# Layer-norm moments of the first stage moved in part from VectorE to GpSimd, with its weight preparation and row stores reordered

## What is computed

```python
h = maximum(_layernorm(x), 0)              # (x - m) / sqrt(v + 1e-5)
Wh = h @ W;  e = leaky_relu(Wh @ a[:128] + (Wh @ a[128:]).T, 0.2)
att = softmax(where(adj > 0, e, -9e15), axis=1)
x = x + gru(att @ Wh, h)                   # gates from w_ih, w_hh, b_ih, b_hh
h = maximum(_layernorm(x), 0)
x = x + adj @ (h @ W1.T + b1)              # adj is 8192 x 8192, zeros and ones
```

## Time and profile before

| | |
|---|---|
| median of 3 runs | 1555.94 us (1554.92 to 1555.95) |
| the profiled execution's own time | 1554.47 us |
| its span | 1552.9 us |
| busy: TensorE | 1485.6 us (96%) |
| busy: VectorE | 1386.0 us (89%) |
| busy: ScalarE | 1369.6 us (88%) |
| busy: GpSimd | 136.2 us (9%) |
| mean DMA rate | 324 GB/s |

### The profile page before, as it was taken

How to read it: one execution, slowest core, us unless ns; L and a number is a source line. 1 busy time by engine, 2 the same in 40 slices (tenths; PEclk the granted TensorE clock), 3 DMA queues, 4 the chain that set the end, 5 groups by cost and what they waited for, 6 DMA issues and landing times.

```text
span 1552.9 us, 35381 instructions
## 1 busy us (share of the span) xinstructions
PE 1485.6 (96%) x13262; PEld 1304.4 (84%) x13262; DVE 1386.0 (89%) x2256; ACT 1369.6 (88%) x1972; POOL 136.2 (9%) x98
## 2 busy tenths in 40 slices
PE   5477999999999999999999999999999999999998
PEld 5356888888888888888888888888888888888887
DVE  8997999999999999999999999997579877766684
ACT  5779999999999999999999999996185998777785
POOL 5000011001100010001000100010000000000000
PEclk9778999999999999999999999999999999999999
DMA  8858999999999999999999999996386999888860
GB/s 314 298 204 332 365 350 360 352 366 353 355 357 370 352 349 353 374 351 357 359 365 345 362 362 355 349 360 265 122 354 238 408 361 352 308 304 310 321 228 16
DMA packets 96380, 502.93 MB, mean 324 GB/s; under 512 B 9599, under 2 KB 38985, under 8 KB 75337
## 3 DMA queue, kind: packets, MB, share of 16 engines
q1 hardware_dynamic: 78328, 444.54, 76.1%
q10 hardware_dynamic: 18000, 57.74, 9.8%
HBM read 418.32 MB, written 83.92 MB: 323 GB/s over the span
## 4 chain that ended last, share of the span: by engine, by line
PE 92%; DVE 5%; ACT 1%; issue 1%; DMA 0%; POOL 0%; DVEq 0%; ACTq 0%
PE ACC L1014 57%; PE ACC L1104 29%; PE GP L1040 2%; PE GP L1043 2%; PE GQ L1061 1%; ACT M L506 1%; DVE M L659 1%; DVE JK L642 1%; DVE TB L733 1%; DVE AE L728 1%; DVE JK L728 1%; PE TG L1027 0%; PE TG L1050 0%; DVE JK L646 0%; DVE M L751 0%
## 5 line engine op out<-in xcount | busy, mean ns | idle before, releaser
L1014 PE MATMUL ACC<-TB,M 128*128 128x258 f16 x8192 | 927.2, 275 | 41.8 <-DVE M L751 30.7
L1014 PEld LDWEIGHTS ACC<-TB,M 128*128 128x128 fp8e4 x8192 | 804.5, 98 | 150.7 <-issue 43.2
L506 ACT ACTIVATE M<-SB,dsteep 128x256 fp8e4<-128x256 f32 x1273 | 526.2, 538 | 0.0
L516 ACT ACTIVATE JK<-X 128x3328 uint8<-128x3328 uint32 x124 | 373.2, 3010 | 0.0
L692 DVE TENSOR_SCALAR Y<-X 128x4096 fp8e4<-128x4096 f32 x128 | 291.9, 2280 | 5.9 <-DMA X<-in_adjb_dram 5.5
L605 ACT ACTIVATE TB<-TB 128x8192 uint8<-128x8192 fp8e4 x32 | 225.0, 7030 | 76.5 <-DVE TB L890 71.7
L1104 PE MATMUL ACC<-WG,X 128*128 128x256 f16 x2048 | 225.5, 273 | 0.0
L1104 PE MATMUL ACC<-WG,TB 128*128 128x256 f16 x2048 | 225.4, 273 | 0.0
L1104 PEld LDWEIGHTS ACC<-WG,X 128*128 128x128 fp8e4 x2048 | 200.4, 98 | 23.2
L1104 PEld LDWEIGHTS ACC<-WG,TB 128*128 128x128 fp8e4 x2048 | 200.4, 98 | 23.1
L743 DVE TENSOR_SCALAR M<-SB,nd 128x256 fp8e4<-128x256 f32 x775 | 213.7, 345 | 0.0
(11 more groups left out here) (145 smaller groups left out, 786.9 us busy)
## 6 DMA issues: line engine op xcount, KB each, us to landing
X<-in_adjb_dram SPq DMA_DIRECT2D x128, 2048.0 KB, 9.8
mask_bytes<-Y SPq DMA_DIRECT2D x128, 512.0 KB, 5.1
M<-in_adjb_dram ACTq DMA_DIRECT2D x24, 1920.0 KB, 9.8
X<-mask_bytes SPq DMA_DIRECT2D x16, 2048.0 KB, 9.5
TB<-mask_bytes SPq DMA_DIRECT2D x16, 2048.0 KB, 9.1
M<-in_adjb_dram ACTq DMA_DIRECT2D x4, 2048.0 KB, 11.9
M<-in_xb_dram SPq DMA_DIRECT2D x8, 512.0 KB, 8.3
h_rows<-M SPq DMA_DIRECT2D x8, 512.0 KB, 3.9
```

The costliest lines, as they stand in the source:

```text
L506: ins = nc.scalar.activation(rows(mask1(c), jj), SB[u][:, :], ACT.Sigmoid, scale=STEEP, bias=dsteep[:, j:j + 1], saturate=False)
L516: nc.scalar.activation(junk[:, 0:SEEN], X[c % 2][:, 0:SEEN].bitcast(u32), ACT.Sign, accum_out=nz[:, bass.ds(k, 1), at:at + 1].rearrange("p ...
L1014: ins = nc.tensor.matmul(A[t][m][:, 0:2 * TW], rows((mask1, mask2)[m](c), jj)[:, t * P:(t + 1) * P], TB[:, c * JC + jj, m, 0:2 * TW], star ...
```

## The change

In the first stage:

1. VectorE aggregates only groups 0 and 1. Groups 2 to 7 get `bn_stats` alone, and GpSimd combines the halves for two groups at a time (`pair_moments`): mean = half the sum of the two means; variance + epsilon = the sum of the two parts over 128, plus epsilon, plus the square of (even mean - mean); then the power on 16 columns.
2. `bn_stats` of groups 2 and 3 runs behind `normalised(0)`, of 4 and 5 behind `normalised(1)`, of 6 and 7 behind `normalised(3)`. The copy into wext stands behind groups 2 and 3.
3. GpSimd prepares the gate weights only when VectorE has normalised all groups (`p_hd` at 16).
4. SP stores the rows of groups 0, 1 and 2 behind columns 9, 11 and 13, those of groups 3 to 7 behind column 15 and ahead of the second adjacency block. The first adjacency block stays behind column 7.
5. The factor TSCALE enters the exponentials as log(TSCALE) in their offset; VectorE's two multiplications of the tables go.
6. Semaphore `d_hh` is shared with the new GpSimd steps (18 increments), so line 770 waits for 18 more; the judging wait of line 941 drops from 3 to 1.

```diff
@@ sync
                 for k in range(16):
                     sp.wait_ge(p_ht, k + 1)
                     sp.dma_start(ht_d[:, k * 512:(k + 1) * 512], hTq[k % 4]).then_inc(p_htout[k % 4], 16)
-                    if k % 2:
-                        q = k // 2
+                    if k == 7:
+                        sp.dma_start(X[0][:, :], adjb[0, :, :]).then_inc(c_in[0], 16)
+                    for q in range(*((k - 9) // 2, (k - 7) // 2) if 9 <= k < 15 and k % 2 else (3, 8 if k == 15 else 3)):
                         sp.dma_start(h_d[:, q * 8:(q + 1) * 8, :], H[:, q * 8:(q + 1) * 8, :]).then_inc(p_hout, 16)
-                    if k in (7, 15):
-                        b = k // 15
-                        sp.dma_start(X[b][:, :], adjb[b, :, :]).then_inc(c_in[b], 16)
+                    if k == 15:
+                        sp.dma_start(X[1][:, :], adjb[1, :, :]).then_inc(c_in[1], 16)
@@ gpsimd
-                for q in range(4):
+                def pair_moments(p):
+                    at = slice(p * 16, p * 16 + 16)
+                    mean_e, part_e, mean_o, part_o = [stx[:, at, i:i + 1].rearrange("p t k -> p (t k)") for i in (1, 2, 4, 5)]
+                    mean = mvx[:, at, 0:1].rearrange("p t k -> p (t k)")
+                    pool.wait_ge(p_st, 2 * p + 2)
+                    nc.gpsimd.tensor_tensor(px[0], mean_e, mean_o, ALU.add).then_inc(p_ag, 1)
+                    nc.gpsimd.tensor_tensor(px[1], part_e, part_o, ALU.add).then_inc(p_ag, 1)
+                    pool.wait_ge(p_ag, p * 6 - 5)
+                    nc.gpsimd.tensor_scalar(mean, px[0], 0.5, None, ALU.mult).then_inc(p_ag, 1)
+                    pool.wait_ge(p_ag, p * 6 - 4)
+                    nc.gpsimd.tensor_scalar(px[1], px[1], 1.0 / F, EPS, ALU.mult, ALU.add).then_inc(p_ag, 1)
+                    pool.wait_ge(p_ag, p * 6 - 3)
+                    nc.gpsimd.tensor_tensor(px[0], mean_e, mean, ALU.subtract).then_inc(p_ag, 1)
+                    pool.wait_ge(p_ag, p * 6 - 1)
+                    nc.gpsimd.tensor_tensor(px[0], px[0], px[0], ALU.mult).then_inc(p_ag, 1)
+                    pool.wait_ge(p_ag, p * 6)
+                    nc.gpsimd.tensor_tensor(sdx[:, at], px[1], px[0], ALU.add).then_inc(p_sd, 1)
+                    pool.wait_ge(p_sd, p + 2)
+                    nc.gpsimd.tensor_tensor(rsx[:, at], sdx[:, at], half[:, 0:1].to_broadcast([P, 16]), ALU.pow).then_inc(
+                        p_rs, 2)
+
+                for q in range(2):
                     deviation(q)
+                pair_moments(1)
                 pool.wait_ge(p_wa, 1)
...
-                for q in range(4, 8):
-                    deviation(q)
+                for p in range(2, 4):
+                    pair_moments(p)
+                pool.wait_ge(p_hd, 16)
                 pool.wait_ge(wt_in, 64)
@@ vector
                 stats(0)
+                stats(1)
                 for q in range(8):
-                    if q < 7:
-                        stats(q + 1)
                     normalised(q)
+                    if q in (0, 1, 3):
+                        for ahead in range(q + q % 2 + 2, q + q % 2 + 4):
+                            halves_stats(ahead)
                     if q == 0:
                         dve.wait_ge(p_wa, 1)
                         nc.vector.tensor_copy(wext[:, 0:2], GP[:, 0:2]).then_inc(p_ab, 1)
@@
-                nc.vector.tensor_scalar(kt[:, 0:1], kt[:, 2:3], -1.0, None, ALU.mult)
-                nc.vector.tensor_scalar(kt[:, 1:2], kt[:, 2:3], -SLOPE, None, ALU.mult).then_inc(p_k, 1)
+                nc.vector.tensor_scalar(kt[:, 0:1], kt[:, 2:3], -1.0, math.log(TSCALE), ALU.mult, ALU.add)
+                nc.vector.tensor_scalar(kt[:, 1:2], kt[:, 2:3], -SLOPE, math.log(TSCALE), ALU.mult, ALU.add).then_inc(p_k, 1)
@@ table_product
                     if i == 0:
-                        for n, table in enumerate((bt, dt_)):
-                            dve.wait_ge(p_exp, n + 1)
-                            nc.vector.tensor_scalar(table, table, TSCALE, None, ALU.mult).then_inc(t_sc, 1)
                         dve.wait_ge(p_one, 2)
                         for b in range(2):
                             dve.wait_ge(p_htout[b], 64)
-                        dve.wait_ge(t_sc, 2)
+                    if i < 2:
+                        dve.wait_ge(p_exp, i + 1)
```

More of the change, by code:

```diff
@@ L1 @@
 from contextlib import ExitStack
+import math
 import concourse.bass as bass
@@ L151, in binary_adjacency @@
         nmx = JK[:, 670:670 + NT]
+        px = [JK[:, 740 + 20 * i:740 + 20 * i + 16] for i in range(2)]
         BG = X1[0].bitcast(bf16)
@@ L206, in binary_adjacency @@
         d_hh, d_hl = sem("d_hh"), sem("d_hl")
+        p_ag = d_hh
         g_sum = p_wa
@@ L638, in _, with halves_stats @@
             def _(dve):
-                def stats(q):
+                def halves_stats(q):
                     dve.wait_ge(p_x[q], 16)
@@ L643, in stats @@
                     ins.then_inc(p_st, 1)
+                def stats(q):
+                    halves_stats(q)
                     dve.wait_ge(p_st, q + 1)
@@ L769, in gate_step @@
                     if halving:
-                        dve.wait_ge(d_hh, qh + 1)
+                        dve.wait_ge(d_hh, 18 + qh + 1)
                         nc.vector.tensor_tensor(HH[:, 1, :], HT[u], HH[:, 0, :], ALU.subtract).then_inc(d_hl, 1)
@@ L940, in judge @@
                 def judge():
-                    dve.wait_ge(k_w, 3)
+                    dve.wait_ge(k_w, 1)
                     nc.vector.tensor_reduce(bad[:, 3:4], GP[:, 0:1], AX.X, ALU.max).then_inc(k_v, 1)
```

## The result

The changed kernel took 1557.97 us in the median of 12 runs (1555.21 to 1560.35), the one before 1556.05 in 12 runs (1554.80 to 1558.05). The ratio is 1.0016, 95% interval [1.0008, 1.0023]: slower by 1.9 us between the medians, 2.5 by the ratio, and so within the 0.2% that the prediction called no change. The profiled execution after is the longest of the twelve, 1560.35 us with a span of 1558.8.

The account below looks back on a forecast made before the run. An entry of some 126 us paced by VectorE, ScalarE and stores, then a TensorE-bound body. Compute side -0.9 us, but late row stores gate the masks: sum +1.4 on 1555.94, forecast 1557.4; 8-in-10 range 1554.7 to 1560.3.

Parts of the forecast that it names:

- The last row store so lands at 47.7 + 5.1 = 52.8: Entry: four row stores moved behind the first adjacency load add 5.1 us at 411 GB/s to the last landing.
- The first masks start at 52.85: everything behind it moves with them: Line 506: masks wait for the last row store, start 1.4 to 1.5 us later than 51.39, and delay everything behind.
- The load: First adjacency load: issued at 28.8, landing at 37.5 as before, with column 12 waiting behind it until 38.25.
- It will run 3.1 us later: Copy at line 672, behind two more groups of statistics: 14.8 instead of 11.64; columns and features start 3.1 us late.
- The pair: GpSimd's moments for two groups: seven small operations at 0.45 us and a power of 1.9, 5.0 us in all.
- the port rule: VectorE and GpSimd share a port: each small operation could wait one multiplication more, 1.9 us a pair, 6.9 in all.
- Saved there: 2.5 us: VectorE's last normalised group: moving the gate weights' preparation away cuts its multiplications from 4.08 to 1.6 us.
- 0.4 is left of the 8: VectorE ends about 8 us sooner, but column 12's wait leaves only 0.4 us of that at the columns' end.
- Dropping the scaling: Table scaling behind the columns: two instructions, 0.49 us, come off the path to the first masks.
- 1 (stores in time): Last row store lands 1.5 us or more sooner, compute side rules: -0.9 us, 1555.0; chance 0.22.
- 3 (GpSimd sets the pace): Pair 3's power holds groups 6 and 7; at 9 us a pair, +6 us, 1562; chance 0.08.
- 2 (second load late): Second adjacency load, margin 0.7 us, also makes VectorE wait at line 692: +3 to +4 us, 1559.5; chance 0.10.

Follow-up runs that it names:

- own_waits: Changed kernel, each quarter of row block 0's masks waiting only for the row stores of the two groups it overwrites; ratio 1.0002 to the kernel before.
- rows_late: Kernel before with only the new order of the row stores; ratio 1.0004 to the kernel before.
- load_sooner: Changed kernel with the first adjacency load behind column 5 instead of 7; ratio 1.0018 to the kernel before.
- after_again: The changed kernel unedited, profiled and timed again; ratio 1.0006 to the kernel before.
- rows_back: Changed kernel with row stores and adjacency loads back in their old places; ratio 1.0020 to the kernel before.
- best: Changed kernel with early wext copy, bias chain last, first load behind column 5, second ahead of last row stores, stores reordered, masks' waits split; ratio 0.9992 to before.
- bias_last: Changed kernel with GpSimd's bias chain behind pair 3 instead of pair 1, SP's wait for it at column 13; ratio 1.0016 to the kernel before.

## Why the prediction was right, and where not

The forecast was 1557.4 and no change; measured 1557.97. The term that carried it, masks gated by the last row store, is shown: forecast 52.85, measured 52.39 and 52.65, and it goes when the wait goes (own_waits) and comes when the stores alone are moved (rows_late).

- *"The last row store so lands at 47.7 + 5.1 = 52.8"*: measured 52.3 and 52.5. I counted four stores moved behind the first load and took the engines for full from there on. In the changed kernel they were (share 1.05 and 1.04 from 38 to 46 us), and the count of bytes comes out: 37.1 + 15.3 = 52.4. As a rule for other store or load positions it fails. By it rows_late would have had its last store at 35.9 + 15.3 = 51.2 and had it at 52.6; load_sooner at 33.7 + 16.6 = 50.3 (two more column stores stand behind its load) and had it at 54.5. The 9.9 to 10.4 us behind the last column fit all seven kernels. That both counts give one figure in the changed kernel was luck.
- *"The first masks start at 52.85: everything behind it moves with them"*: 1.0 to 1.3 us came on, but 0.3 of it was regained before the combination (0.68 and 0.92 left there), since the table products that the high parts wait for were ready by then. Forecast for the entry +1.4, measured +0.7 to +0.9 at the first product. It did not reach the body one for one in each profile either: the body started 0.8 us later than before in the changed kernel and 1.8 in after_again. The medians differ by 1.9 and 1.3 us, so that the total came within 0.6 us of the forecast is in part chance.
- *The load*: issued at 27.85 and 28.4, not 28.8, landed at 37.1 and 37.4 (forecast 37.5); column 12 met it as said, with 0.7 and 1.4 us of wait (1.85 forecast). Last column's end 42.5 to 42.9 (42.9 forecast).
- *"It will run 3.1 us later"*: the copy did (14.58), the columns' start too. What I missed is that GpSimd's first power would have held group 2 anyway, so undoing it gains 0.3 to 0.5.
- *The pair*: 5.3 us against 5.0 (pairs 2 and 3: 4.9 and 5.1). Both parts were off and cancelled: the power on 16 columns took 2.93 us, not 1.9, since it grew with the columns; the small operations took 2.4, not 3.1. By the port rule that I weighed it would have been 6.9; the measured pair lies at the row's price.
- *"Saved there: 2.5 us"* at group 7: shown on VectorE, worth 0.15 at the last column. *"0.4 is left of the 8"*: 0.5 to 0.8 was.
- *Dropping the scaling*: 0.3 us at the masks, not 0.49, and nothing at the first product.
- Rivals: 1 (stores in time) and 3 (GpSimd sets the pace) did not happen; 2 (second load late) is there as soon as the first gate is taken away (1.02 us in own_waits).

What stays open: the first measurement's ratio is 1.0016, after_again's 1.0006 for the same kernel. The entry explains 0.7 to 0.9 us. The rest of the first figure fits late loads in single executions like the profiled one, but only that one was profiled.

## What to carry to other kernels

When stores are moved to the end of a stage, find who waits for the last of them and count from its issue as well as from the queue's total, and take the later; the total alone holds only while the engines stay full. Here 2.6 MB behind the last column landed 1.9 us after the next stage was ready. Before making a producer faster, look at the next wait its consumer has; freeing GpSimd here lengthened a DMA stall, the granted clock of TensorE fell behind it, and the masks came 1.9 us later. And a wait for all of a set of transfers, where the work needs one, is worth splitting first.

## What the runs showed of the hardware

- Issuing a 512 KB store from SP took 0.43 us for the last one of the kernel before. Of five in a row in the changed kernel the average was 0.9 us, and the last took 1.16 and landed 6.0 us after its issue; six in a row in `best` averaged 0.5.
- GpSimd's power -0.5 took 1.65 us on 128x8 and 2.93 on 128x16: by these two, 0.16 us a column over 0.4.
- In the stage of f32 matmuls, with ScalarE's columns stalled for 2.4 to 3.7 us and TensorE idle meanwhile, the granted clock of a four-microsecond stretch behind it was 0.68 (rows_back), 0.66 (bias_last) and 0.80 (load_sooner), between the two levels, and two columns stood 2.9 to 3.1 us apart instead of 2.1. With the 1.4 us stall of after_again it was 1.00.
